# Causal attention on one Trainium2 core: query-side scores in two pairs of PSUM banks, six row maxima a head, the split of the maximum on GpSimd

## The chip, the core and the metric

The kernel runs on one core of a Trainium2 chip. The metric is device time in microseconds (us); three runs of the kernel before gave 2903.61, 2900.68 and 2903.25, so the median is 2903.25. Engines are named as in the profile: PE is TensorE's matrix multiplication, PEld its weight load, DVE VectorE, ACT ScalarE, POOL GpSimd, SP SyncE.

## The reference, cut to what matters

The model is a convolution-style block (linear attention and an MLP), a causal softmax attention, and a feed-forward block with grouped quantization. The change touches the attention alone. Its arithmetic is this:

```python
k = (x @ Wk).reshape(B, H, T, hs)     # B = 32, H = 6, T = 1024, hs = 16
q = (x @ Wq).reshape(B, H, T, hs)
v = (x @ Wv).reshape(B, H, T, hs)
wei = jnp.einsum('bhtd,bhsd->bhts', q, k) * scale
wei = jnp.where(mask, wei, -jnp.inf)
wei = jax.nn.softmax(wei, axis=-1)
out = jnp.einsum('bhts,bhsd->bhtd', wei, v).reshape(B, T, C)
```

That is 192 heads of 1024 rows and 16 columns. A head is cut into 8 blocks of 128 rows; below and on the diagonal there are 36 blocks of 128 x 128 scores.

## The kernel before, in words

The program has a preparation, `conv_block`, `causal_attention` and `project_and_ffn`, one after the other. In `causal_attention` each head's scores are computed twice. First **on the query side**: rows are queries, and DVE takes the maximum of each row straight from PSUM. The negated maximum is split into two bf16 parts (high part and rest), turned by PE, copied by ACT and sent by a DMA into two spare rows of the queries' stack. Then **on the key side**: rows are keys, the two spare rows subtract the maximum inside the matmul, ACT takes the exponential from PSUM into SBUF, and PE multiplies with the values.

Every engine runs the same software pipeline, written out by hand: a `body(i)` for the iteration i, in which the stages of different heads stand together; heads are i for loading and spreading (POOL), i-2 for the query side (PE, DVE), i-3 for turning the maximum, i-4 and i-5 for the key side, i-5 for the output. The loop body is six iterations long (`SLOTS`). 190 iterations hold both a head's query side and a head's key side. Inside a `body`, PE goes through nine steps u = 0 to 8:

- Query units (`QUNITS`, line 853 in the profile): twelve a head. A unit is one PSUM bank of `at_ps_queries`: a strip of up to 512 keys for one query block, or four diagonal blocks followed by one matmul of 512 columns that adds the mask (line 857). `QSTEP` gives the step of each: 1, 2, 2, 3, 4, 4, 5, 6, 6, 7, 7, 8. The text calls the units Q0 to Q11. There are four banks (`QBANKS`); a unit waits until DVE has reduced the unit four before it (`unit_max`).
- Key units (line 868): nine a head, K0 to K8, one a step, in two banks (`KBANKS`). The key unit of a step is the last thing in it. K0 and K1 are the diagonal, K2 to K5 are one matmul of 512 columns each, K6 to K8 two matmuls with 512 together. In iteration i, steps 2 to 8 do K0 to K6 of head i-4, and steps 0 and 1 of the next iteration K7 and K8 of it. A key unit waits until ACT has done the exponential (`probs`, line 928) of the unit two before it. 
- Values (line 888): a batch of five units at step 0 and one of four at step 4.
- The turning of the maxima (line 834) at step 2 and of the output (line 843) at step 8, ahead of K6. The second waits for ACT's copy of the output (line 937), which ACT does after the exponential of K3.

DVE goes through the twelve units in order (one `tensor_reduce` each, line 982); before the last one it divides the output of head i-5 (lines 969 and 972); after it come the maximum over the parts (line 986) and the split (lines 990 and 992). POOL waits for the head's rows (`at_stacks`), spreads them (lines 803 to 816) and masks the diagonal probabilities of head i-4 (lines 820 and 822). SP issues the DMAs in order: rows of head i once head i-1 is spread, the transposing DMA of head i-1, the maximum's rows, the output's two.

Of the kernel before, what the change touches and what calls it, by code (L numbers as in the profile page):

```python
# [8 lines left out]
ALU = mybir.AluOpType  # L9
# [674 lines left out]
def causal_attention(nc, w, rows, rows_stored, att):  # L684
# [11 lines left out]
    WIDE = NU - DIAG  # L696
    SLOTS = 6
    BATCHES = {4: (0, 1, 2, 3, 4), 8: (5, 6, 7, 8)}
    QBANKS, KBANKS = 4, 2
    QDIAG = [[(qb, qb * P, P) for qb in range(g, g + HALF)] for g in (0, HALF)]  # L700
    QUNITS = [[(1, 0, P)], [(2, 0, 2 * P)], QDIAG[0], [(4, 0, BANK)], [(5, 0, BANK)], [(3, 0, 3 * P)], [(6, 0, BANK)],
              [(5, BANK, P)], QDIAG[1], [(7, BANK, 3 * P)], [(6, BANK, 2 * P)], [(7, 0, BANK)]]
    NQ = len(QUNITS)
    QSTEP = [1, 2, 2, 3, 4, 4, 5, 6, 6, 7, 7, 8]
    LAG = 11
    VALUES_LAG = 14
    MAX_TURN, MAX_COPY, OUT_COPY, OUT_TURN = 2, 3, 5, 8
    OUT_QUNIT = 11
    VW = 32
    with ExitStack() as ctx:  # L710
        def sb(name, shape, dt=FP32):
# [2 lines left out]
        def pb(name, shape, dt=FP32):  # L714
            return ctx.enter_context(nc.psum_tensor("at_ps_" + name, shape, dt))
# [21 lines left out]
        ONE = sb("one", [P, 1, 1])  # L737
        OT = sb("out_t", [P, 2 * P])
        AT = sb("att", [P, SLOTS, TILES, HD])
        pq = pb("queries", [P, QBANKS, BANK])  # L740
        pk = pb("keys", [P, KBANKS, BANK])
        pv = pb("values", [P, 2 * P])
        bank = pb("turn", [P, BANK])
# [12 lines left out]
        with nc.Block() as block:  # L756
# [30 lines left out]
            def _(pool):  # L787
# [7 lines left out]
                pool.wait_ge(S["one_set"], 1)  # L795

                def body(i, r, lap, on):
                    if on(0):
                        pool.wait_ge(loaded[r], _dmas(lap, r, 0, SLOTS))
                        _above(pool.wait_ge, S["values"], NU * (i - SLOTS + 1))  # L800
                        _above(pool.wait_ge, turned_in[r], _dmas(lap, r, SLOTS, SLOTS))
                        v = ST[:, r, :, PW:PW + HD].bitcast(FP32)
                        pool.tensor_tensor(V[:, r, :, 0:HD], v, ONE[:, :, :].broadcast_to([P, TILES, HD]), ALU.mult)  # L803
                        k, q = ST[:, r, :, 0:PW], ST[:, r, :, PW + HD:PACK]
                        ks, qs = (SPREAD[:, r, m, :, 0:STACK].bitcast(U32) for m in range(2))
                        h = HD // 2
                        pool.tensor_copy(ks[:, :, 0:3 * h], k)
                        pool.tensor_copy(ks[:, :, 3 * h:5 * h], k[:, :, 0:2 * h])
                        pool.tensor_copy(ks[:, :, 5 * h:6 * h], k[:, :, 0:h])
                        pool.tensor_copy(qs[:, :, 0:3 * h].rearrange("p t (m d) -> p t m d", m=3),  # L810
                                         q[:, :, 0:h].rearrange("p t (m d) -> p t m d", m=1)
                                         .broadcast_to([P, TILES, 3, h]))
                        pool.tensor_copy(qs[:, :, 3 * h:5 * h].rearrange("p t (m d) -> p t m d", m=2),
                                         q[:, :, h:2 * h].rearrange("p t (m d) -> p t m d", m=1)
                                         .broadcast_to([P, TILES, 2, h]))
                        pool.tensor_copy(qs[:, :, 5 * h:6 * h], q[:, :, 2 * h:3 * h]).then_inc(S["spread"], 1)
# [11 lines left out]
            def _(pe):  # L828
# [17 lines left out]
                def query_scores(h, r, lap, u):  # L846
                    slot = (r - 2) % SLOTS
                    if u == 0:
                        pe.wait_ge(turned_in[slot], _dmas(lap, r, 2, SLOTS))
                    _above(pe.wait_ge, S["unit_max"], NQ * h + u - QBANKS + 1)  # L850
                    c0 = 0
                    for qb, k0, n in QUNITS[u]:
                        mm = pe.matmul(pq[:, u % QBANKS, c0:c0 + n], QT[0:STACK, slot, qb * P:(qb + 1) * P],  # L853
                                       KT[0:STACK, slot, k0:k0 + n], start=(c0 == 0), stop=True, skip_group_check=True)
                        c0 += n
                    if len(QUNITS[u]) > 1:
                        mm = pe.matmul(pq[:, u % QBANKS, :], w["ident_bf"][:, :], w["mask_queries"][:, :],
                                       start=False, stop=True, skip_group_check=True)
                    mm.then_inc(S["q_scores"], 1)

                def key_scores(h, slot, lands, u):
# [79 lines left out]
            def _(dve):  # L941
# [20 lines left out]
                dve.tensor_tensor(w["w2"][:, :, 0:GROUPS * gs2], A2[:, :, :], B2[:, :, :], ALU.subtract)  # L962

                def body(i, r, lap, on):
                    for u, blocks in enumerate(QUNITS):
                        if u == OUT_QUNIT and on(5):
                            q = (r - 5) % SLOTS
                            dve.wait_ge(S["out_turned"], i - 4)
                            dve.reciprocal(RC[:, :], out_ps[:, :, HD]).then_inc(S["recip"], 1)
                            dve.wait_ge(S["recip"], i - 4)  # L970
                            _above(dve.wait_ge, stored[q], 2 * _dmas(lap, r, 5 + SLOTS, SLOTS))
                            dve.tensor_tensor(AT[:, q, :, :], out_ps[:, :, 0:HD], _bcast(RC[:, :], 2, HD),
                                              ALU.mult).then_inc(S["out_ready"], 1)
                        if on(2):
                            dve.wait_ge(S["q_scores"], NQ * (i - 2) + u + 1)
                            qb, k0, n = blocks[0]
                            if len(blocks) > 1:
                                peaks, scores = MX[:, r % 2, qb:qb + len(blocks), 2], pq[:, u % QBANKS, :].rearrange(
                                    "p (t n) -> p t n", n=P)
                            else:  # L980
                                peaks, scores = MX[:, r % 2, qb, k0 // BANK:k0 // BANK + 1], pq[:, u % QBANKS, 0:n]
                            dve.tensor_reduce(peaks, scores, AX.X, ALU.max).then_inc(S["unit_max"], 1)  # L982
                    if on(2):
                        dve.wait_ge(S["unit_max"], NQ * (i - 1))
                        _above(dve.wait_ge, S["max_parts"], i - 2)
                        dve.tensor_reduce(NM[:, :], MX[:, r % 2, :, :], AX.X, ALU.max,
                                          negate=True).then_inc(S["head_max"], 1)
                        dve.wait_ge(S["head_max"], i - 1)
                        _above(dve.wait_ge, S["max_turned"], i - 3)
                        dve.tensor_copy(MP[:, r % 2, 0:TILES], NM[:, :]).then_inc(S["max_high"], 1)  # L990
                        dve.wait_ge(S["max_high"], i - 1)
                        dve.tensor_tensor(MP[:, r % 2, TILES:2 * TILES], NM[:, :], MP[:, r % 2, 0:TILES],
                                          ALU.subtract).then_inc(S["max_parts"], 1)
                _pipeline(dve, body, NHEADS, 7, SLOTS)


# [426 lines left out]
```

## Time and profile before

| | |
|---|---|
| median of three runs | 2903.25 us |
| span of the profiled execution | 2901.5 us |
| attention (query side of the first head to the values of the last) | about 1009 to 2424 us of the span |
| PE busy / PEld / DVE / ACT / POOL, whole span | 94% / 58% / 79% / 70% / 40% |
| one head in the middle of the attention | 7.285 us (1100 us hold 151 heads) |

The profile is of one execution. Busy shares are those of instruction records. The records of PE overlap: matmuls are pipelined, so the distance between the starts of two matmuls tells how long one holds the array, and its duration in the record (0.38 us for 512 columns) is longer than that (0.22 us). Idle time in front of an instruction is shown with the instruction that ended it. A few per cent of the matmul records are missing, among them nearly all of the mask matmul, line 857.

### The profile page before, as it was taken

To read this page: it belongs to the slowest core of one execution; us is meant where nothing else is said; L and a number is where in the kernel's file an instruction comes from. 1 tells how busy PE (TensorE), PEld (TensorE's weight loads), DVE (VectorE), ACT (ScalarE), POOL (GpSimd) and SP (SyncE) were. 2 spreads that over 40 slices of the span, in tenths; PEclk is the share of its full clock that TensorE was granted. 3 is DMA by queue.
4 is the path that set the end of the run, shared out by engine and by line. 5 is a ranking of instruction groups with operands and counts; after the bars stand their busy time and mean duration, and the time that the engine had idled before them with its cause. 6 is when DMAs were issued, how large, how long until landed. Compare 5 with 4: busy or idle time off the path is not lost. (4 is left out here: it accounts for less than half of the span.)

```text
span 2901.5 us, 86028 instructions
## 1 busy us (share of the span) xinstructions
PE 2730.6 (94%) x28924; PEld 1685.7 (58%) x29306; DVE 2300.3 (79%) x4585; ACT 2020.8 (70%) x3943; POOL 1153.0 (40%) x1999
## 2 busy tenths in 40 slices
PE   4999999999999499999999999999999997899996
PEld 2555555555554266666666666666666664455553
DVE  3577676676765499999999999999999994678997
ACT  2677777777776267777777777777777774577775
POOL 1144443444434434444444444444444441224445
PEclk9999999999999699999999999999999998999998
DMA  1113223232332466666666666666666663334555
GB/s 34 44 55 115 90 100 114 76 114 85 105 114 85 128 118 119 116 118 118 118 118 118 118 118 118 118 117 117 117 117 117 118 117 86 99 105 132 147 142 154
DMA packets 923408, 316.04 MB, mean 109 GB/s; under 512 B 848785, under 2 KB 906418, under 8 KB 923314
## 3 DMA queue, kind: packets, MB, share of 16 engines
q1 hardware_dynamic: 921970, 313.59, 47.8%
q8 instruction: 60, 0.98, 0.1%
q10 hardware_dynamic: 1344, 1.18, 0.1%
q14 instruction: 34, 0.28, 0.0%
HBM read 113.35 MB, written 99.88 MB: 73 GB/s over the span
## 5 line engine op out<-in xcount | busy, mean ns | idle before, releaser
L982 DVE TENSOR_REDUCE at_unit_max<-at_ps_queries 128x1 f32<-128x512 f32 (+4 forms) x2304 | 1135.9, 550 | 86.0 <-PE at_ps_queries L853 83.5
L928 ACT ACTIVATE at_probs<-at_ps_keys 128x512 f32<-128x512 f32 x1344 | 743.3, 603 | 388.9 <-PE at_ps_keys L868 384.5
L853 PE MATMUL at_ps_queries<-at_turned 96*128 96x128 bf16 (+3 forms) x3456 | 635.1, 275 | 30.6 <-DMA at_turned<-at_spread 29.4
L868 PE MATMUL at_ps_keys<-at_turned 128*128 128x128 bf16 x3453 | 648.4, 275 | 13.3 <-ACT at_probs L928 1.7
L803 POOL TENSOR_TENSOR at_v<-at_stacks,at_one 128x128 f32<-128x128 f32 x192 | 76.7, 399 | 818.5 <-DMA at_stacks<-qkv_rows 818.5
L888 PE MATMUL at_ps_values<-at_probs,at_v 128*32 128x128 f32 x10752 | 373.4, 276 | 6.5 <-ACT at_probs L928 6.5
L868 PEld LDWEIGHTS at_ps_keys<-at_turned 128*128 128x128 bf16 x3456 | 238.0, 97 | 239.5 <-ACT at_probs L928 88.3
L853 PEld LDWEIGHTS at_ps_queries<-at_turned 96*128 96x128 bf16 x3456 | 289.7, 98 | 122.0 <-DMA at_turned<-at_spread 31.3
L888 PEld LDWEIGHTS at_ps_values<-at_probs,at_v 128*32 128x32 f32 x10752 | 269.5, 109 | 120.6 <-ACT at_diag_probs L928 70.2
L928 ACT ACTIVATE at_diag_probs<-at_ps_keys 128x512 f32<-128x512 f32 x384 | 208.7, 595 | 8.5 <-PE at_ps_keys L868 5.6
L822 POOL TENSOR_SCALAR_AFFINE_SELECT at_diag_probs<-at_diag_probs 128x1024 f32<-128x1024 f32 x192 | 210.3, 1095 | 0.0
L576 PE MATMUL cb_ps_hidden<-cb_xn_t,fc 96*128 96x512 f32 x384 | 186.2, 615 | 8.4 <-ACT cb_hidden_t L557 8.4
L487 POOL TENSOR_TENSOR cb_o_hat<-cb_o,cb_o_scale 128x768 f32<-128x768 f32 x32 | 48.1, 1502 | 357.0 <-DVE cb_o_scale L403 357.0
L637 PE MATMUL cb_ps_out<-cb_hidden_t,fc 128*96 128x512 f32 x384 | 176.2, 594 | 0.0
L1121 PE MATMUL ff_ps_hidden<-ff_xn_t,w 97*128 97x512 f32 x360 | 171.0, 609 | 1.8 <-ACT ff_xn_t L1236 1.8
L557 ACT ACTIVATE cb_hidden_t<-cb_ps_hidden,fc_bias 128x512 f32<-128x512 f32 x192 | 128.5, 686 | 59.3 <-PE cb_ps_hidden L576 58.9
L1210 ACT ACTIVATE ff_hidden<-ff_ps_hidden 128x512 f32<-128x512 f32 x180 | 104.6, 597 | 93.2 <-PE ff_ps_hidden L1121 93.2
L467 DVE SCALAR_TENSOR_TENSOR cb_o<-cb_q_norm_v,cb_ps_hidden 128x768 f32<-128x768 f32 x32 | 30.6, 955 | 165.8 <-PE cb_ps_hidden L663 165.8
L1273 POOL TENSOR_TENSOR ff_scale<-ff_var_sums,ff_minus_half 128x8 f32<-128x8 f32 x30 | 49.5, 1650 | 247.0 <-DVE ff_var_sums L1359 247.0
L1313 DVE TENSOR_REDUCE ff_max<-ff_hidden 128x1 f32<-128x1024 f32 x90 | 109.5, 1217 | 36.3 <-ACT ff_hidden L1210 36.3
L576 PEld LDWEIGHTS cb_ps_hidden<-cb_xn_t,fc 96*128 96x128 f32 x384 | 66.1, 193 | 101.2 <-ACT cb_hidden_t L557 71.4
L637 PEld LDWEIGHTS cb_ps_out<-cb_hidden_t,fc 128*96 128x96 f32 x384 | 62.9, 164 | 102.0 <-issue 102.0
(214 smaller groups left out, 4967.4 us busy)
## 6 DMA issues: line engine op xcount, KB each, us to landing
qkv_rows<-cb_packed SPq DMA_DIRECT2D x32, 1536.0 KB, 8.3
at_stacks<-qkv_rows SPq DMA_DIRECT2D x192, 256.0 KB, 3.3
cb_x<-in_x_dram SPq DMA_DIRECT2D x32, 384.0 KB, 3.7
cb_x_again<-in_x_dram SPq DMA_DIRECT2D x32, 384.0 KB, 4.5
x_after_conv<-cb_x SPq DMA_DIRECT2D x32, 384.0 KB, 5.0
attention_rows<-at_att SPq DMA_DIRECT2D x384, 32.0 KB, 2.2
ff_att_rows<-attention_rows SPq DMA_DIRECT2D x32, 384.0 KB, 4.5
ff_x<-x_after_conv SPq DMA_DIRECT2D x128, 96.0 KB, 2.4
```

The lines of the kernel that those rows point to most:

```text
L557: act.activation(HT[:, r, k, a * BANK:(a + 1) * BANK], pf[:, a * BANK:(a + 1) * BANK], ACT.Silu, bias=w["fc1_bias"][:, k:k + 1]).then_inc( ...
L576: pe.matmul(pf[:, a * BANK:(a + 1) * BANK], w["fc1"][:, k * P:(k + 1) * P], XNT[:, a * BANK:(a + 1) * BANK], start=True, stop=True).then_i ...
L637: pe.matmul(po[0:C, half], w["fc2"][:, k, :], HT[:, q, k, half], start=(k == 0), stop=False)
L822: pool.affine_select(out=blocks, in_=blocks, compare_op=ALU.is_ge, fill=0.0, base=0, pattern=[[0, TILES], [1, P]], channel_multiplier=-1). ...
L853: mm = pe.matmul(pq[:, u % QBANKS, c0:c0 + n], QT[0:STACK, slot, qb * P:(qb + 1) * P], KT[0:STACK, slot, k0:k0 + n], start=(c0 == 0), stop ...
L868: mm = pe.matmul(pk[:, bank_k, c0:c0 + n * P], KT[:, slot, kb * P:(kb + 1) * P], QT[:, slot, q0 * P:(q0 + n) * P], start=(c0 == 0), stop=True,
L888: mm = pe.matmul(pv[row:row + VW, col:col + P], V[:, slot, kb, :], probs[:, c0:c0 + P], start=(v == 0), stop=True, skip_group_check=True)
L928: act.activation(probs, pk[:, (slot * NU + k) % KBANKS, :], ACT.Exp, scale=scale).then_inc(S["probs"], 1)
L982: dve.tensor_reduce(peaks, scores, AX.X, ALU.max).then_inc(S["unit_max"], 1)
L1121: pe.matmul(pf[:, a * BANK:(a + 1) * BANK], w["w1"][:, k * P:(k + 1) * P], XNT[:, a * BANK:(a + 1) * BANK], start=True, stop=True).then_in ...
L1210: act.activation(Y1[:, n % SLOTS1, k, a * BANK:(a + 1) * BANK], pf[:, a * BANK:(a + 1) * BANK], ACT.Copy).then_inc(S["y1_copied"], 1)
L1313: dve.tensor_reduce(G1[:, n // GB % 2, c:c + 1], Y1[:, n % SLOTS1, k, :], AX.X, ALU.max, apply_absolute_value=True).then_inc(S["y1_max"], 1)
```

## The change

The query units become five, Q0 to Q4, each in a pair of neighbouring banks (1024 columns), and there are two pairs. Q0 holds all eight diagonal blocks with both masks, Q1 the first 512 keys of query blocks 4 and 5, Q2 those of 6 and 7, Q3 the mixed strips (384 + 128 in each bank), Q4 256 and 256. Their steps are 0, 0, 1, 3, 5. A unit waits until the unit two before it is reduced. DVE reduces four units with one instruction each and Q3 with two. DVE's split moves to POOL, as the first thing of the next iteration (for head i-3), and the division of the output moves behind the maximum over the parts.

```diff
-    QBANKS, KBANKS = 4, 2
+    QPAIRS, KBANKS = 2, 2
-    QUNITS = [[(1, 0, P)], [(2, 0, 2 * P)], QDIAG[0], [(4, 0, BANK)], [(5, 0, BANK)], [(3, 0, 3 * P)], [(6, 0, BANK)],
-              [(5, BANK, P)], QDIAG[1], [(7, BANK, 3 * P)], [(6, BANK, 2 * P)], [(7, 0, BANK)]]
+    QUNITS = [QDIAG, [[(4, 0, BANK)], [(5, 0, BANK)]], [[(6, 0, BANK)], [(7, 0, BANK)]],
+              [[(3, 0, 3 * P), (1, 0, P)], [(7, BANK, 3 * P), (5, BANK, P)]], [[(2, 0, 2 * P), (6, BANK, 2 * P)]]]
+    QMAXIMA = [[(0, 8, 1, 2, P, 0, P)], [(4, 6, 1, 0, BANK, 0, BANK)], [(6, 8, 1, 0, BANK, 0, BANK)],
+               [(3, 8, 4, 1, BANK, 0, 3 * P), (1, 6, 4, 1, BANK, 3 * P, P)], [(2, 7, 4, 1, 2 * P, 0, 2 * P)]]
-    QSTEP = [1, 2, 2, 3, 4, 4, 5, 6, 6, 7, 7, 8]
+    QSTEP = [0, 0, 1, 3, 5]
...
@@ pool body @@
+                    if on(3):
+                        q = (r - 3) % SLOTS % 2
+                        pool.wait_ge(S["head_max"], i - 2)
+                        _above(pool.wait_ge, S["max_turned"], i - 4)
+                        pool.tensor_tensor(MP[:, q, 0:TILES], NM[:, :], ONE[:, :, 0].broadcast_to([P, TILES]), ALU.mult
+                                           ).then_inc(S["max_high"], 1)
+                        pool.wait_ge(S["max_high"], i - 2)
+                        pool.tensor_tensor(MP[:, q, TILES:2 * TILES], NM[:, :], MP[:, q, 0:TILES],
+                                           ALU.subtract).then_inc(S["max_parts"], 1)
...
@@ query_scores on PE @@
-                    _above(pe.wait_ge, S["unit_max"], NQ * h + u - QBANKS + 1)
+                    before = MAXDONE[u - QPAIRS] if u >= QPAIRS else MAXDONE[u - QPAIRS + NQ] - NMAX
+                    _above(pe.wait_ge, S["unit_max"], NMAX * h + before)
+                    pair = pq[:, (NQ * r + u) % QPAIRS, :]
...
@@ dve body @@
-                        dve.wait_ge(S["head_max"], i - 1)
-                        _above(dve.wait_ge, S["max_turned"], i - 3)
-                        dve.tensor_copy(MP[:, r % 2, 0:TILES], NM[:, :]).then_inc(S["max_high"], 1)
-                        dve.wait_ge(S["max_high"], i - 1)
-                        dve.tensor_tensor(MP[:, r % 2, TILES:2 * TILES], NM[:, :], MP[:, r % 2, 0:TILES],
-                                          ALU.subtract).then_inc(S["max_parts"], 1)
+                    if on(5):
+                        q = (r - 5) % SLOTS
+                        dve.wait_ge(S["out_turned"], i - 4)
+                        dve.reciprocal(RC[:, :], out_ps[:, :, HD]).then_inc(S["recip"], 1)
...
```

**PE, steps 5 to 8 of an iteration.** In the kernel before, from K3 to the first matmul of K6 (`at_ps_keys` at line 868 is a key unit, `at_ps_queries` at line 853 a query unit, `at_ps_turn` the turned output):

```order
L868 MATMUL at_ps_keys<-at_turned 128x512 [waits at_probs]
L853 MATMUL at_ps_queries<-at_turned 128x128 [waits at_unit_max] x2
L853 MATMUL at_ps_queries<-at_turned 128x128 x3
L857 MATMUL at_ps_queries<-mask_queries,ident_bf 128x512
L868 MATMUL at_ps_keys<-at_turned 128x512 [waits at_probs]
L853 MATMUL at_ps_queries<-at_turned 128x384 [waits at_unit_max]
L853 MATMUL at_ps_queries<-at_turned 128x256 [waits at_unit_max]
L868 MATMUL at_ps_keys<-at_turned 128x512 [waits at_probs]
L853 MATMUL at_ps_queries<-at_turned 128x512 [waits at_unit_max]
L843 MATMUL at_ps_turn<-ident,at_out_t 128x128 [waits at_max_copied,at_out_ready,at_out_copied]
L843 MATMUL at_ps_turn<-ident,at_out_t 128x128
L868 MATMUL at_ps_keys<-at_turned 128x384 [waits at_probs]
```

The same place now, from K2 on (line 884 is a key unit, 868 a query unit, 855 the turned output):

```order
L884 MATMUL at_ps_keys<-at_turned 128x512 [waits at_probs]
L868 MATMUL at_ps_queries<-at_turned 128x256 [waits at_unit_max]
L868 MATMUL at_ps_queries<-at_turned 128x256
L884 MATMUL at_ps_keys<-at_turned 128x512 [waits at_probs] x3
L855 MATMUL at_ps_turn<-ident,at_out_t 128x128 [waits at_max_copied,at_out_ready,at_out_copied]
L855 MATMUL at_ps_turn<-ident,at_out_t 128x128
L884 MATMUL at_ps_keys<-at_turned 128x384 [waits at_probs]
L884 MATMUL at_ps_keys<-at_turned 128x128
```

The query matmuls that stood between K3, K4, K5 and K6 are gone from there, and K3, K4 and K5 follow each other; the query matmuls stand at steps 0, 1 and 3 now.

**DVE, one head.** Before, the row maxima (line 982), the output (969, 972), the maximum over the parts (986) and the split (990, 992):

```order
L982 TENSOR_REDUCE at_unit_max<-at_ps_queries 128x1 [waits at_q_scores] x2
L982 TENSOR_REDUCE at_unit_max<-at_ps_queries 128x4 [waits at_q_scores]
L982 TENSOR_REDUCE at_unit_max<-at_ps_queries 128x1 [waits at_q_scores] x5
L982 TENSOR_REDUCE at_unit_max<-at_ps_queries 128x4 [waits at_q_scores]
L982 TENSOR_REDUCE at_unit_max<-at_ps_queries 128x1 [waits at_q_scores] x2
L969 RECIPROCAL at_recip<-at_ps_turn 128x8 [waits at_out_turned]
L972 TENSOR_TENSOR at_att<-at_ps_turn,at_recip 128x128 [waits at_recip]
L982 TENSOR_REDUCE at_unit_max<-at_ps_queries 128x1 [waits at_q_scores]
L986 TENSOR_REDUCE at_neg_max<-at_unit_max 128x8 [waits at_max_parts,at_unit_max]
L990 CAST at_max_parts<-at_neg_max 128x8 [waits at_max_turned,at_head_max]
L992 TENSOR_TENSOR at_max_parts<-at_neg_max,at_max_parts 128x8 [waits at_max_high]
```

Now, one head on DVE:

```order
L989 TENSOR_REDUCE at_unit_max<-at_ps_queries 128x8 [waits at_q_scores]
L989 TENSOR_REDUCE at_unit_max<-at_ps_queries 128x2 [waits at_q_scores] x3
L989 TENSOR_REDUCE at_unit_max<-at_ps_queries 128x2
L989 TENSOR_REDUCE at_unit_max<-at_ps_queries 128x2 [waits at_q_scores]
L993 TENSOR_REDUCE at_neg_max<-at_unit_max 128x8 [waits at_max_parts,at_unit_max]
L998 RECIPROCAL at_recip<-at_ps_turn 128x8 [waits at_out_turned]
L1001 TENSOR_TENSOR at_att<-at_ps_turn,at_recip 128x128 [waits at_stored1,at_recip]
```

Twelve reductions became six, the two instructions of the split left the engine, and the output's two stand behind the maximum over the parts.

## Rows read from the trace of the kernel before

**Rows 1.** Busy time by engine, 1200 to 2300 us: the middle of the attention.

```profile
core 0: us, PE busy (x) PEld busy (x) DVE busy (x) ACT busy (x) POOL busy (x), PEclk, DMA share, GB/s
1200.00:2300.00 1100.00, 1077.53 (x16740) 725.62 (x17033) 1009.65 (x2566) 791.32 (x1659) 451.35 (x1355) 1.00 0.64 117
```

**Rows 2.** Who waited for whom, 1200 to 2300 us: total, times, longest.

```profile
POOL at_v L803 <- DMA at_stacks<-qkv_rows: 648.6, 151, 5.0
...
PEld at_ps_keys L868 <- ACT at_probs L928: 70.5, 376, 0.2
DVE at_unit_max L982 <- PE at_ps_queries L853: 60.3, 176, 0.4
```

**Rows 3.** Timeline of PE over one head: start, length, line, tile, form, count.

```profile
1623.61 0.39 PE L868 MATMUL at_ps_keys<-at_turned 128*128 128x512 bf16 x1
1623.84 0.38 PE L853 MATMUL at_ps_queries<-at_turned 96*128 96x512 bf16 x1
1624.06 0.38 PE L868 MATMUL at_ps_keys<-at_turned 128*128 128x512 bf16 x1
1624.28 0.44 PE L853 MATMUL at_ps_queries<-at_turned 96*128 96x128 bf16 x5
1624.78 0.38 PE L868 MATMUL at_ps_keys<-at_turned 128*128 128x512 bf16 x1
1624.99 0.43 PE L853 MATMUL at_ps_queries<-at_turned 96*128 96x384 bf16 x2
1625.26 0.38 PE L868 MATMUL at_ps_keys<-at_turned 128*128 128x512 bf16 x1
1625.48 0.38 PE L853 MATMUL at_ps_queries<-at_turned 96*128 96x512 bf16 x1
1625.70 0.38 PE L843 MATMUL at_ps_turn<-ident,at_out_t 128*128 128x128 f32 x2
1625.94 0.39 PE L868 MATMUL at_ps_keys<-at_turned 128*128 128x384 bf16 x2
1626.27 1.30 PE L888 MATMUL at_ps_values<-at_probs,at_v 128*32 128x128 f32 x40
1627.50 0.39 PE L868 MATMUL at_ps_keys<-at_turned 128*128 128x256 bf16 x2
...
1628.56 0.22 PE L834 MATMUL at_ps_turn<-ident_bf,at_max_parts 128*128 128x128 bf16 x1
1628.61 0.39 PE L868 MATMUL at_ps_keys<-at_turned 128*128 128x128 bf16 x4
...
1630.79 0.39 PE L868 MATMUL at_ps_keys<-at_turned 128*128 128x512 bf16 x1
```

**Rows 4.** Timeline of ACT over the same head.

```profile
1624.04 1.09 ACT L928 ACTIVATE at_probs<-at_ps_keys 128x512 f32<-128x512 f32 x2 [0.97 <-PE at_ps_keys L868]
1625.01 0.39 ACT L937 ACTIVATE at_out_t<-at_ps_values 128x256 f32<-128x256 f32 x1
1625.27 1.70 ACT L928 ACTIVATE at_probs<-at_ps_keys 128x512 f32<-128x512 f32 x3
1627.92 1.09 ACT L928 ACTIVATE at_probs<-at_ps_keys 128x512 f32<-128x512 f32 x2 [0.96 <-PE at_ps_keys L868]
```

**Rows 5.** Two heads earlier, timelines of ACT and PEld: the exponential of K2, the load for K4.

```profile
1609.45 1.09 ACT L928 ACTIVATE at_probs<-at_ps_keys 128x512 f32<-128x512 f32 x2 [1.06 <-PE at_ps_keys L868]
...
1610.10 0.10 PEld L868 LDWEIGHTS at_ps_keys<-at_turned 128*128 128x128 bf16 x1 [0.18 <-ACT at_probs L928]
```

**Rows 6.** DVE by form, 1200 to 2300 us: busy us, mean ns, idle before.

```profile
L982 DVE TENSOR_REDUCE at_unit_max<-at_ps_queries 128x1 f32<-128x512 f32 x603 | 399.4, 683 | 51.2 <-PE at_ps_queries L853 51.2
...
L982 DVE TENSOR_REDUCE at_unit_max<-at_ps_queries 128x1 f32<-128x128 f32 x302 | 86.3, 286 | 9.1 <-PE at_ps_queries L853 9.1
```

**Rows 7.** Timeline of DVE: five reductions of 1792 columns together, then the reciprocal.

```profile
1624.26 2.28 DVE L982 TENSOR_REDUCE at_unit_max<-at_ps_queries 128x1 f32<-128x512 f32 x5 [0.40 <-PE at_ps_queries L853]
1626.45 0.20 DVE L969 RECIPROCAL at_recip<-at_ps_turn 128x8 f32<-128x8 f32 x1
```

**Rows 8.** Timeline of POOL over the same head: two of its small operations.

```profile
1621.87 0.40 POOL L803 TENSOR_TENSOR at_v<-at_stacks,at_one 128x128 f32<-128x128 f32 x1 [4.30 <-DMA at_stacks<-qkv_rows]
...
1623.63 0.20 POOL L820 TENSOR_TENSOR at_tick<-at_one 128x1 f32<-128x1 f32 x1
```

**Rows 9.** Busy time and granted clock, 985 to 1015 us: the start of the attention.

```profile
985.00:1015.00 30.00, 5.78 (x25) 2.63 (x27) 14.15 (x42) 0.00 (x0) 13.11 (x28) 0.50 0.62 168
```

## What I predicted before the run

> **What bounds the kernel now.** I first read the busy times over the middle of the attention [rows 1]. The reader is to see two engines near their limit: PE at 1077.5 of 1100 us and DVE at 1009.7. ACT has 791 and POOL 451. POOL waits for the rows of a head 151 times in that stretch, once a head [rows 2], so a head takes 1100 / 151 = 7.285 us. All of this change that can matter is what it does to that number, 190 times (the iterations that have both a query side and a key side).
>
> Which of the two engines sets it? The list of waits says so [rows 2]: DVE stood waiting for PE's query scores for 60.3 us, while no row has PE waiting for DVE; PE's weight loads waited for ACT's exponentials for 70.5 us, at most 0.2 at a time, much of it hidden under the matmul that was still running. So PE leads, DVE follows with 0.4 us of air a head, and the only engine that ever holds PE is ACT.
>
> Then I read PE by its starts [rows 3]. A matmul of 512 columns holds the array for 0.22 us (1623.84 to 1624.06). From K2 (1623.61) to the next head's K2 (1630.79) are 7.18 us, and in them the starts follow each other without a hole: such a head is pure PE work. The mean is 0.1 above it. So **PE can gain about 0.1 us a head at most, whatever DVE is spared**, and it can lose as much as its waits grow.
>
> Where is PE nearly waiting? Between K2 and K6 [rows 3, 4]. ACT begins the exponential of K2 at 1624.04, that of K3 0.49 later (two take 1.09, so one is 0.60 long), then copies the output (1625.01 to 1625.40), then that of K4 at 1625.27, which ends 0.60 later at 1625.87. K6 needs that last one, because there are two key banks, and K6 starts at 1625.94. How fast PE goes on after an exponential is seen two heads earlier [rows 5]: exponential of K2 from 1609.45 to 1610.05, load for K4 at 1610.10, so 0.05 us. **ACT needs 2.31 us from the start of K2 to that of K6** (0.43 + 0.49 + 0.49 + 0.25 + 0.60 + 0.05), and PE's own work between them takes 2.33 (1625.94 - 1623.61). The two are even: PE's query matmuls just fill the time that ACT needs for its exponentials.
>
> **The change part by part.**
>
> *The same matmuls, in another order.* The query side has 36 blocks and two masks before and after, so PE's work stays at 7.18 us a head. What moves is where it stands. Between K2 and K6 the kernel before had Q6, then Q7 and Q8 with its mask (1624.28 to 1624.78, 0.50), Q9 and Q10 (1624.99 to 1625.26, 0.27), Q11 (1625.48 to 1625.70, 0.22) [rows 3]. Now only Q4 stands there, with the 512 columns that Q6 had. So 0.50 + 0.27 + 0.22 = **0.99 us of PE's work leaves this stretch**. What is left in it is 2.33 - 0.99 = 1.34 us, but ACT still needs 2.31. Counted from K2's start, PE is at K4 at 0.67 and may start at 1.08 (exponential of K2: 0.43 + 0.60 + 0.05); K5 may start at 1.57, the turned output at 1.84 (copy ends at 1.79), K6 at 2.31. Four holes, of 0.41, 0.27, 0.05 and 0.23 us, together 0.97 but for rounding (2.31 - 1.34). The stretch stays at 2.3 us with a hole of 0.97, and the 0.99 are added to the rest of the head, which was solid PE work before (4.85 us from K6 to the next K2). Nothing there has air to take them: **+0.99 us a head**.
>
> *K0 after the second query pair.* ACT starts on K7 0.42 after K7's start (1627.50, 1627.92) [rows 3, 4], ends 0.60 later, and K0 may go 0.05 after that: 1.07. PE now gets there after K7 (0.22), Q2 (0.44), K8 (0.22) and the turned maximum (0.05 to 0.10) [rows 3]: 0.93 to 0.98. That is a new hole of about 0.09 us; before, the way from K7 to K0 took 1.11. Where ACT begins 0.09 later, as it did at 1609.45 [rows 5], it is 0.18. Lower end 0. I take **+0.09**.
>
> *Six reductions fewer, the split gone from DVE.* A reduction of 512 columns lasts 683 ns and one of 128 lasts 286 [rows 6], so a column costs 1.03 ns. Five with 1792 columns took 1626.45 - 1624.26 = 2.19 us from start to start [rows 7]; less 1792 x 1.03 = 1.85 leaves 0.34, so what each instruction adds is 0.07 us, not the 0.15 that its record seems to say, since the records overlap. Six fewer free 0.4 us of DVE, and the two small ones of the split some tenths more. All of it lies on an engine that was waiting already. Worth: 0.
>
> *Two pairs in the place of four banks.* This adds waits of PE for DVE, so I follow one. Q0 holds PE for 2048 columns, 0.88 us; its scores are seen 0.16 later (0.38 - 0.22) and DVE starts 0.04 after that (Q6: 1623.84 + 0.38, DVE at 1624.26) [rows 3, 7]. A reduction of 1024 columns isn't in this stage; from 683 ns and 1.03 a column it is 1.21 us. So Q0 is reduced at 0.88 + 0.16 + 0.04 + 1.21 = 2.29. Q2, which needs that pair, comes after Q1 (0.44), the batch of five values (1626.27 to 1627.50, 1.23) and K7 (0.22): at 2.77. It has 0.48 us of air. Q1 is reduced 1.14 later, at 3.43, and Q3 comes at 2.77 + 0.44 + 0.22 + 0.1 + 0.3 = 3.8. Q4 and the next Q0 have over a microsecond. Worth: 0; from below it can't be a gain, since no PE wait for DVE was there; from above, see the rivals.
>
> *The split on POOL.* Two operations on 128x8; the nearest rows are 0.20 us for 128x1 and 0.40 for 128x128 [rows 8], so 0.4 to 0.8 with the wait between them. They stand at the head of POOL's iteration, before the spreading of the next head, where POOL has waited 4.3 us for the rows from memory [rows 2, 8]. Queued behind the new wait are the spreading, SP's transposing DMA after it, and the diagonal mask that the values wait for. DVE's maximum over the parts is ready about a step after Q4, well before the rows land. PE turns the maximum at step 2 of the next iteration, over 3 us later. Worth: 0, with that wait of 4.3 us as cover.
>
> *The division behind the maximum.* On DVE, which has air: 0.
>
> **Sum.** 0.99 + 0.09 = 1.08 us a head; 190 heads give +205 us. Against the profiled execution, 2901.5 + 205 = 3106.5, and the median stands 1.75 above its span: 3108. The fill of the pipeline, where DVE alone is slow, gives back a microsecond or two: **3106 us**. Bounds of this case: if the holes between K2 and K6 are a tenth smaller and K0 has none, 0.90 a head, 3074; if ACT is late at each place (0.18 at K0, and a few hundredths at each of the hand-overs), 1.25, 3141.
>
> **The rivals.**
>
> *DVE was the bound, and the kernel gets faster.* For it: DVE is busy 92% of the time and its chain gets shorter by well over half a microsecond. The Trainium skill ("Perfetto Trace Analysis", "Identifying the Most-Contended Engine") says that matmul busy time isn't a fair measure of TensorE and the share of weight loads is, while a busy share is fair for VectorE; by that rule DVE with 92% would stand ahead of PE with 66% of weight loads [rows 1], and the change would pay. Against it: DVE waits for PE and never PE for DVE. Its price: PE's own 7.18 us stays, so at most 0.1 a head is gained, 190 x 0.1 = 20 us, 2883. It also needs the holes at K4 to K6 not to come. Chance 0.06.
>
> *The change does nothing to the time.* If ACT got to its exponentials sooner than I read, or if what I call solid work between K6 and K2 had a microsecond of air in it, the two would cancel: 2898 to 2909. The starts in rows 3 speak against the air. Chance 0.04.
>
> *Half of it.* ACT is busy 72% of the time only, so some of the holes may close by a shift that I don't see: +0.5 us a head, 2998. Chance 0.04.
>
> *The pairs bind as well.* If a reduction over two banks takes longer than 1.21 us by more than the 0.48 of air (eight groups of 128, or strips with a step of 512, might go slower than a single bank), PE waits at Q2 and Q3 too: half a microsecond a head on top, 3106 + 95 = 3200. Chance 0.04.
>
> *The clock falls.* At the start of the attention, where PE was busy 5.8 of 30 us, the granted clock is 0.50, so 1.2 GHz; in the middle it is 1.00, 2.4 GHz [rows 1, 9]. Now PE would have holes of half a microsecond again and again. One head in eight at half the clock would cost 7 / 8 of a microsecond a head, +165, 3270. The Trainium skill ("TensorE: Matmul & The Clock Gate", "A second HAM failure mode: psum-queue depth-cycling") tells of a kernel whose small pauses between groups of matmuls in cycling PSUM banks made the clock go back and forth; by that rule this case would be likelier than I make it. The holes are short beside 24 us of idleness in rows 9. Chance 0.02.
>
> **How the numbers follow.** Forecast 0.80, DVE bound 0.06, no change 0.04, half 0.04, pairs 0.04, clock 0.02. The range holds the forecast's bounds, 3074 to 3141, with some more below for holes that partly close, down to 3060, and 3145 above; the rivals, 0.20 in all, are outside. Faster by over 0.2%: 0.06; within 0.2%, about what a measurement can tell from no change: 0.04; slower: 0.90.
>
> **What would show it.** In the new profile a head in the middle of the attention should last about 8.36 us; PE should have holes ahead of K4, K5 and K6 ended by ACT's exponentials, together near a microsecond; DVE's waits for PE should grow from 0.4 us to nearly 2 a head, its busy share fall to about 70%; a reduction of 1024 columns should last 1.21 us; ACT's stretch from the exponential of K2 to that of K4 should keep its 1.23 us; POOL's two new operations should have no one waiting for them; the granted clock should stay at 1.00. I am wrong if PE waits for `at_unit_max`, if K4 comes without a hole, or if the time from K6 to the next K2 stays near 4.9 us and doesn't grow to 5.9.

## The result, and the profile after

The changed kernel takes 3120.59 us (median of four runs, 3119.75 to 3121.93); the kernel before, run beside it, 2901.97. The ratio is 1.0753, with a 95% interval of 1.0738 to 1.0768: slower by 7.5%. The forecast was 3106 us, with a range of 3060 to 3145. The span of the profiled execution is 3118.9 us, 217.4 more than before.

The first two views are of the changed kernel, 1200 to 2300 us, and answer to [rows 1, 2]: busy time by engine, and who waited for whom (total us, times, longest).

```profile
1200.00:2300.00 1100.00, 1014.96 (x14654) 619.07 (x14785) 806.52 (x1175) 699.58 (x1436) 448.49 (x1437) 1.00 0.56 102
```

```profile
POOL at_v L815 <- DMA at_stacks<-qkv_rows: 492.5, 131, 4.4
...
PEld at_ps_keys L884 <- ACT at_probs L944: 214.3, 521, 0.7
DVE at_unit_max L989 <- PE at_ps_queries L873: 107.3, 131, 1.1
DVE at_recip L998 <- PE at_ps_turn L855: 103.0, 130, 0.9
POOL at_max_parts L805 <- DVE at_neg_max L993: 86.1, 130, 0.7
...
DVE at_unit_max L989 <- PE at_ps_queries L868: 60.9, 130, 0.5
...
PE at_ps_queries L868 <- DVE at_unit_max L989: 20.6, 130, 0.2
```

POOL's wait comes 131 times where it came 151 times, so a head takes 1100 / 131 = 8.4 us in place of 7.285. DVE fell from 92% to 73% busy and waits three times a head (107.3 + 103.0 + 60.9 = 271 us, 2.1 a head, where it was 0.4). The weight loads of the key units wait three times as long for ACT (214.3 us against 70.5). The clock is 1.00 as before.

A finer measure, which the experiments below use too: the view of one tile gives the first and the last turned maximum, 191 heads apart. Before they are at 1015.9 and 2408.3, so a head is 7.29 us; now at 1019.7 and 2624.9, **8.40 us**, 1.11 more. 191 x 1.114 = 213 of the 217 us lie there. The lengths of single heads repeat every six heads: most often 7.18 us before (up to 7.50), most often 8.29 now (up to 8.68). The timelines show one head of the shortest kind in each kernel.

Where in the head? Timeline of PE over one head, against [rows 3] (start, length, line, tile, form, count; line 884 is a key unit, 868 a query unit, 873 the mask, 904 values, 855 the turned output, 846 the turned maximum):

```profile
1626.91 0.38 PE L868 MATMUL at_ps_queries<-at_turned 96*128 96x256 bf16 x2 [0.16 <-DVE at_unit_max L989]
1627.13 0.38 PE L884 MATMUL at_ps_keys<-at_turned 128*128 128x512 bf16 x1
1627.76 0.88 PE L884 MATMUL at_ps_keys<-at_turned 128*128 128x512 bf16 x2 [0.25 <-ACT at_probs L944]
1628.53 0.44 PE L855 MATMUL at_ps_turn<-ident,at_out_t 128*128 128x128 f32 x2
1629.02 0.39 PE L884 MATMUL at_ps_keys<-at_turned 128*128 128x384 bf16 x2
...
1631.89 0.39 PE L884 MATMUL at_ps_keys<-at_turned 128*128 128x256 bf16 x2
1632.12 0.60 PE L868 MATMUL at_ps_queries<-at_turned 96*128 96x512 bf16 x2
1632.56 0.38 PE L884 MATMUL at_ps_keys<-at_turned 128*128 128x128 bf16 x2
1632.78 0.22 PE L846 MATMUL at_ps_turn<-ident_bf,at_max_parts 128*128 128x128 bf16 x1
1632.97 0.40 PE L884 MATMUL at_ps_keys<-at_turned 128*128 128x128 bf16 x4
...
1635.20 0.39 PE L868 MATMUL at_ps_queries<-at_turned 96*128 96x256 bf16 x2 [0.16 <-DVE at_unit_max L989]
```

The weight loads of the same stretch, with the idle time before each; the first is K2's:

```profile
1626.68 0.10 PEld L884 LDWEIGHTS at_ps_keys<-at_turned 128*128 128x128 bf16 x1 [0.20 <-issue]
...
1627.76 0.10 PEld L884 LDWEIGHTS at_ps_keys<-at_turned 128*128 128x128 bf16 x1 [0.64 <-ACT at_probs L944]
1628.25 0.10 PEld L884 LDWEIGHTS at_ps_keys<-at_turned 128*128 128x128 bf16 x1 [0.39 <-ACT at_probs L944]
1628.53 0.20 PEld L855 LDWEIGHTS at_ps_turn<-ident,at_out_t 128*128 128x128 f32 x2 [0.18 <-ACT at_out_t L953]
1629.02 0.11 PEld L884 LDWEIGHTS at_ps_keys<-at_turned 128*128 128x128 bf16 x2 [0.29 <-ACT at_probs L944]
```

And ACT, against [rows 4]:

```profile
1627.11 1.08 ACT L944 ACTIVATE at_probs<-at_ps_keys 128x512 f32<-128x512 f32 x2 [0.59 <-PE at_ps_keys L884]
1628.08 0.39 ACT L953 ACTIVATE at_out_t<-at_ps_values 128x256 f32<-128x256 f32 x1
1628.35 1.70 ACT L944 ACTIVATE at_probs<-at_ps_keys 128x512 f32<-128x512 f32 x3
```

K2's matmul has no record here, but its weight load stands at 1626.68, 0.23 ahead of Q4 as in [rows 3]; ACT begins on it 0.43 later, as before. That also explains the "0.16 <-DVE" at Q4, and with it the one row of the list in which PE seems to wait for DVE (20.6 us): the gap is the missing matmul, not a wait. From the starts: PE is done with K3 at 1627.35 and starts K4 at 1627.76, a hole of 0.41; K5 follows at 1628.25, a hole of 0.27; the turned output at 1628.53, 0.06; K6 at 1629.02, 0.25. **Together 0.99 us of holes, each ended by ACT.** K2 to K6 takes 2.34 us, as before (2.33). From K6 to the next K2 (its load is at 1634.97) it is 5.95, where it was 4.85.

### The profile page after: what moved, and what is told of

It reads as the page before. It is cut to its first block and busy times, and to the rows that moved or that the text cites. A ratio compares the mean times of both kernels' runs of the same rounds, so it can differ in the third digit from the quotient of the medians.

```text
span 3118.9 us, 82755 instructions
## 1 busy us (share of the span) xinstructions
PE 2849.3 (91%) x29113; PEld 1670.1 (54%) x29306; DVE 2196.9 (70%) x3049; ACT 2042.0 (65%) x3943; POOL 1236.3 (40%) x2383
## 5 line engine op out<-in xcount | busy, mean ns | idle before, releaser
L989 DVE TENSOR_REDUCE at_unit_max<-at_ps_queries 128x2 f32<-128x1024 f32 (+4 forms) x1152 | 1054.8, 955 | 269.4 <-PE at_ps_queries L873 168.4
L944 ACT ACTIVATE at_probs<-at_ps_keys 128x512 f32<-128x512 f32 x1344 | 764.1, 604 | 579.4 <-PE at_ps_keys L884 564.7
L884 PE MATMUL at_ps_keys<-at_turned 128*128 128x128 bf16 (+3 forms) x3264 | 597.5, 269 | 90.6 <-ACT at_probs L944 54.5
L868 PE MATMUL at_ps_queries<-at_turned 96*128 96x128 bf16 (+3 forms) x3456 | 573.2, 274 | 69.2 <-DVE at_unit_max L989 33.1
L868 PEld LDWEIGHTS at_ps_queries<-at_turned 96*128 96x128 bf16 x3456 | 282.1, 98 | 153.3 <-DMA at_turned<-at_spread 31.0
L944 ACT ACTIVATE at_diag_probs<-at_ps_keys 128x512 f32<-128x512 f32 x384 | 228.2, 595 | 9.8 <-PE at_ps_keys L884 6.4
L998 DVE RECIPROCAL at_recip<-at_ps_turn 128x8 f32<-128x8 f32 x192 | 39.9, 208 | 166.5 <-PE at_ps_turn L855 166.5
L873 PE MATMUL at_ps_queries<-mask_queries,ident_bf 128*128 128x512 bf16 x383 | 147.2, 384 | 0.0
```

Of the source, the lines that this page charges most:

```text
L868: mm = pe.matmul(pair[:, c0:c0 + n], QT[0:STACK, slot, qb * P:(qb + 1) * P], KT[0:STACK, slot, k0:k0 + n], start=(c0 == b * BANK), stop=Tr ...
L873: mm = pe.matmul(pair[:, b * BANK:(b + 1) * BANK], w["ident_bf"][:, :], w["mask_queries"][:, :], start=False, stop=True, skip_group_check= ...
L884: mm = pe.matmul(pk[:, bank_k, c0:c0 + n * P], KT[:, slot, kb * P:(kb + 1) * P], QT[:, slot, q0 * P:(q0 + n) * P], start=(c0 == 0), stop=True,
L944: act.activation(probs, pk[:, (slot * NU + k) % KBANKS, :], ACT.Exp, scale=scale).then_inc(S["probs"], 1)
L989: dve.tensor_reduce(MX[:, r % 2, first:last:every, part], scores, AX.X, ALU.max).then_inc(S["unit_max"], 1)
```

## The experiments

For each, "a head" is the distance between the first and the last turned maximum over 191; the kernel before has 7.29, the changed one 8.40. Ratios are to the kernel before, on the same chip.

### The changed kernel's order in the kernel before (e2)

```diff
-    QSTEP = [1, 2, 2, 3, 4, 4, 5, 6, 6, 7, 7, 8]
+    QSTEP = [0, 0, 0, 0, 1, 1, 2, 3, 3, 4, 4, 5]
```

> The kernel before (four banks, twelve reductions, split on DVE) with one table altered: the steps of the twelve query units become 0, 0, 0, 0, 1, 1, 2, 3, 3, 4, 4, 5, so that only one unit of 512 columns stands between K2 and K6, as in the changed kernel. Theory: the same holes come at K4, K5, K6, a head lasts about 8.3 to 8.4 us, the kernel 3090 to 3125. Rival (pairs, fewer instructions or POOL's split are what costs): it stays near 2902, at most 1% above.

Measured: 3207.88 us, ratio 1.1054 (1.1036 to 1.1072), a head 8.88. With four banks, twelve reductions and the split on DVE the loss is there, and larger. Timeline of PE (line 868 is now the key unit, 853 the query unit, 888 values):

```profile
1701.78 0.39 PE L868 MATMUL at_ps_keys<-at_turned 128*128 128x512 bf16 x1
1702.01 0.38 PE L853 MATMUL at_ps_queries<-at_turned 96*128 96x512 bf16 x1
1702.23 0.38 PE L868 MATMUL at_ps_keys<-at_turned 128*128 128x512 bf16 x1
1702.86 0.88 PE L868 MATMUL at_ps_keys<-at_turned 128*128 128x512 bf16 x2 [0.25 <-ACT at_probs L928]
1703.62 0.44 PE L843 MATMUL at_ps_turn<-ident,at_out_t 128*128 128x128 f32 x2
1704.12 0.39 PE L868 MATMUL at_ps_keys<-at_turned 128*128 128x384 bf16 x2
1704.34 0.55 PE L853 MATMUL at_ps_queries<-at_turned 96*128 96x128 bf16 x6
1705.29 0.39 PE L853 MATMUL at_ps_queries<-at_turned 96*128 96x512 bf16 x1 [0.39 <-DVE at_unit_max L982]
```

K2 to K6 is the same picture: 2.34 us (1701.78 to 1704.12), K4 0.41 late. The last row is what the expectation missed: PE waits for DVE. Counted by columns (Q0 to Q2 and the mask, whose matmul has no record, are 0.61 us) PE is ready for Q3 at 1704.95 and starts it at 1705.29, a hole of 0.34. The bank of Q3 is the one that Q11 of the head before had. The timeline of DVE shows why it isn't free:

```profile
1704.10 0.21 DVE L969 RECIPROCAL at_recip<-at_ps_turn 128x8 f32<-128x8 f32 x1 [2.01 <-PE at_ps_turn L843]
...
1704.55 0.68 DVE L982 TENSOR_REDUCE at_unit_max<-at_ps_queries 128x1 f32<-128x512 f32 x1
```

DVE was not short of time: it stood idle for 2.01 us. In the kernel before, the division of the output stands ahead of the last unit's reduction, and it waits for the turned output at step 8. Q11 was finished at step 5, but DVE reduces it only behind the division, until 1705.23, and Q3 goes on 0.05 later. Eleven reductions then stand in a row on DVE, and a second wait of PE for it comes at step 4 (the load at 1700.55 waited 0.32). The changed kernel has the division behind the maximum and shows no such wait; the division's place was not tested alone. The theory's size was 0.5 us a head too small, its sign and place were right.

### The pairs, with the steps spread (e1)

```diff
-    QSTEP = [0, 0, 1, 3, 5]
+    QSTEP = [1, 3, 5, 7, 8]
```

> The changed kernel with one table altered: the query units go to steps 1, 3, 5, 7, 8 in place of 0, 0, 1, 3, 5. Theory (ACT paces K2 to K6 and the query work that filled this stretch is gone): the stretch gets 1.10 us of query work back in place of 0.22, K4's hole shrinks from 0.4 to about 0.2, and about 0.2 us of a new wait for DVE comes at Q4; a head should last about 7.55 us in place of 8.43, the kernel about 2950 to 2980. Rival (two pairs in place of four banks, or the split on POOL, make the loss): the order does not matter much and the time stays within 1% of 3120.

Measured: 2986.84 us, ratio 1.0290 (1.0272 to 1.0308), a head 7.72. One table gives back 134 of the 219 us. It is 7 us above the upper end that was expected. The two holes that were expected are there, about 0.2 us at K4 (K3's 0.22 ends at 1705.81, K4's load is at 1706.00) and at Q4 0.18 for DVE (ready at 1706.89, started at 1707.07). The trace also shows a hole that was left out, at K1. Timelines of PE and ACT:

```profile
1702.94 0.60 PE L868 MATMUL at_ps_queries<-at_turned 96*128 96x512 bf16 x2
1703.59 0.40 PE L884 MATMUL at_ps_keys<-at_turned 128*128 128x128 bf16 x4
```

```profile
1702.94 0.60 ACT L944 ACTIVATE at_probs<-at_ps_keys 128x512 f32<-128x512 f32 x1 [0.51 <-PE at_ps_keys L884]
```

Q1 is through at 1703.38, K1 starts at 1703.59, 0.05 after the exponential of K8 ends (1703.54). The whole diagonal, 0.88 us, stood between K7 and K8 and made that exponential late.

### Shorter exponentials (e4)

```diff
-                            act.activation(probs, pk[:, (slot * NU + k) % KBANKS, :], ACT.Exp,
+                            n = BANK if k < DIAG else BANK // 2
+                            act.activation(probs[:, 0:n], pk[:, (slot * NU + k) % KBANKS, 0:n], ACT.Exp,
```

> The changed kernel with ACT's exponentials of K2 to K8 over 256 of their 512 columns (the other half is left out and its place in SBUF holds a constant, so this part of the softmax is not computed). PE's work is unchanged. Theory (the holes are the chain of exponentials): an exponential of 256 columns should last 0.39 us in place of 0.60 and follow the one before after 0.26 in place of 0.49; K2 to K6 shrinks from 2.34 to about 1.85 us and K0's hole goes, so a head lasts 7.8 to 7.9 us and the kernel 3000 to 3025. Rival (PE's holes come from DVE, the banks or PE's own order): the time stays within 0.5% of 3120.

Measured: 2994.57 us, ratio 1.0317 (1.0300 to 1.0334), a head 7.74. But for one memset of DVE ahead of the loop, no PE or DVE instruction was altered, and 126 of the 219 us are gone. The time is 5 us below the range expected. Timeline of PE:

```profile
1703.88 0.39 PE L868 MATMUL at_ps_queries<-at_turned 96*128 96x256 bf16 x2 [0.16 <-DVE at_unit_max L992]
1704.11 1.32 PE L884 MATMUL at_ps_keys<-at_turned 128*128 128x512 bf16 x3
1705.32 0.44 PE L855 MATMUL at_ps_turn<-ident,at_out_t 128*128 128x128 f32 x2
1705.60 0.39 PE L884 MATMUL at_ps_keys<-at_turned 128*128 128x384 bf16 x2
```

K2 (0.23 ahead of the first row, 1703.65) to K6 is 1.95 us in this head. By the starts of the weight loads, as a mean over the heads of 1200 to 2300 us, K2 to K6 is 1.88 in place of 2.36, and from the turned maximum to K0 0.19 in place of 0.40; no other stretch of the head changed by more than 0.02. So the 0.66 us a head came back just where PE waited for exponentials, more of it at K0 than was expected.

### DVE's and POOL's parts, alone (e3, e6, e7)

e3 is the changed kernel with the split back on DVE; e7 is the changed kernel with the maxima of Q1 to Q4 taken bank by bank, eleven reductions a head; e6 is the kernel before with the split on POOL:

```diff
@@ e6: the kernel before @@
+                    if on(3):
+                        q = (r - 3) % SLOTS % 2
+                        pool.wait_ge(S["head_max"], i - 2)
...
-                        dve.tensor_copy(MP[:, r % 2, 0:TILES], NM[:, :]).then_inc(S["max_high"], 1)
```

```diff
@@ e7: the changed kernel @@
-    QMAXIMA = [[(0, 8, 1, 2, P, 0, P)], [(4, 6, 1, 0, BANK, 0, BANK)], [(6, 8, 1, 0, BANK, 0, BANK)],
+    QMAXIMA = [[(0, 8, 1, 2, P, 0, P)], [(4, 5, 1, 0, 2 * BANK, 0, BANK), (5, 6, 1, 0, 2 * BANK, BANK, BANK)],
...
```

> The changed kernel with the split of the maximum back on DVE, behind the maximum over the parts. Theory: the split is off the path in either place, so the time is that of the changed kernel, 3120, within 0.3%. Rival (POOL's wait for the maximum delays the spreading and by it the turned scores, or PE's turning of the maximum): the time falls by 1% or more, to 3090 or below.

> The kernel before with nothing but the split of the maximum moved to POOL, as in the change. Theory: DVE gets 0.3 to 0.5 us a head of air that nobody uses, 2890 to 2905, same within 0.3%. Rival 1 (DVE bounded the kernel before): faster by over 0.5%. Rival 2 (the split on POOL costs): slower by over 0.5%.

> The changed kernel with the row maxima of Q1 to Q4 taken bank by bank, so eleven reductions a head in place of six; pairs, waits and steps as they are. Theory: about 0.35 us more on DVE, which waits over 2 us a head, so no effect: 3120 within 0.3%. Rival (the number of reductions counts): slower by 0.35 us a head or more, 3185 or above.

Measured: e3 3118.30 us, ratio 1.0744 (1.0726 to 1.0762); e7 3119.55, 1.0749 (1.0733 to 1.0766); both are the changed kernel's 1.0753. e6 2902.14, 0.9998 (0.9989 to 1.0007), no change at all. So the place of the split moves the time in neither kernel, and the number of reductions doesn't move it in the changed one. (The division's new place on DVE was not tested alone.) What moves is the waits. In e7, the busy times of 1200 to 2300 us show that DVE took the five reductions more in its stride (845.57 us busy where it was 806.52, with PE as before):

```profile
1200.00:2300.00 1100.00, 1014.68 (x14654) 618.93 (x14777) 845.57 (x1830) 699.76 (x1437) 449.73 (x1439) 1.00 0.55 102
```

In e6, the waits of the same stretch show where the time went that DVE was spared, and what the cover of POOL's split is worth in the old order:

```profile
POOL at_max_parts L802 <- DVE at_neg_max L995: 462.2, 151, 3.4
...
POOL at_v L812 <- DMA at_stacks<-qkv_rows: 114.5, 151, 1.2
DVE at_unit_max L991 <- PE at_ps_queries L862: 90.4, 302, 0.4
```

DVE now waits 90.4 us for PE, where it was 60.3 [rows 2].

POOL now stands 3.1 us a head before the maximum, and of the 4.3 us that it waited for the rows 0.8 are left. The move costs nothing, but four fifths of the cover are used up.

### The pairs in an order that fits (e5, e8)

```diff
@@ e5: the changed kernel; the unit of 256 + 256 and that of query blocks 6 and 7 change places @@
-    QSTEP = [0, 0, 1, 3, 5]
+    QSTEP = [(1, 1), (3, 3), (5,), (6, 6), (7, 8)]
...
-                                if QSTEP[nq] == u:
-                                    query_scores(i - 2, r, lap, nq)
+                                for b, step in enumerate(QSTEP[nq]):
+                                    if step == u:
+                                        query_scores(i - 2, r, lap, nq, b)
@@ e8: e5, but @@
-    QSTEP = [(1, 1), (3, 3), (5,), (6, 6), (7, 8)]
+    QSTEP = [(1, 2), (3, 3), (5,), (6, 6), (7, 8)]
```

A pair's two banks may stand at different steps here; all else of the change is in place.

> The changed kernel with its pairs, its six reductions and POOL's split, but other steps: the order is diagonal (step 1), query blocks 4 and 5 (step 3), the unit of 256 + 256 (step 5), the mixed strips (step 6), query blocks 6 and 7 with one bank at step 7 and one at step 8. Theory: 1.10 us of query work stands between K2 and K6, in pieces of 0.22, 0.44, 0.22 and 0.22 that fit between ACT's exponentials, and no unit comes before DVE has freed its pair by more than 0.1 us; a head should last 7.2 to 7.4 us, the kernel 2885 to 2925, so the whole loss is gone with the pairs still in place. Rival (two pairs cost something of their own in any order): it stays above 2950.

> The reordered pairs (e5) with the diagonal's second bank moved from step 1 to step 2, behind K8. In e5 K1 had a hole of 0.14 us, because 0.88 us of diagonal ahead of K8 made the exponential of K8 late, on which K1 waits. Theory (what e5 still loses against the kernel before is order, not the pairs): that hole goes, 0.1 us a head, 2915 to 2930. Rival (the pairs' waits for DVE make the rest): DVE starts on the diagonal later, the waits at the pairs grow by as much, and the time stays at 2940 or above.

Measured: e5 2944.74 us, ratio 1.0146 (1.0130 to 1.0161), a head 7.51, above the expected range; e8 2913.16, ratio 1.0038 (1.0024 to 1.0051), a head 7.33, just below its range. In e5 the hole at K1 was there again, since the diagonal still stood ahead of K8. Timelines of PE and ACT in e5:

```profile
1701.85 0.60 PE L869 MATMUL at_ps_queries<-at_turned 96*128 96x512 bf16 x2
1702.43 0.40 PE L886 MATMUL at_ps_keys<-at_turned 128*128 128x128 bf16 x4
```

```profile
1701.78 0.60 ACT L947 ACTIVATE at_probs<-at_ps_keys 128x512 f32<-128x512 f32 x1 [0.51 <-PE at_ps_keys L886]
```

and the same two units of PE in e8, 0.43 apart, which is Q1's own 0.44:

```profile
1700.51 0.60 PE L869 MATMUL at_ps_queries<-at_turned 96*128 96x512 bf16 x2
1700.94 0.39 PE L886 MATMUL at_ps_keys<-at_turned 128*128 128x128 bf16 x4
```

So 208 of the 219 us came from the order. What is left of the whole change in e8, pairs, six reductions, split and division, is 0.4%, or 0.04 us a head. One small wait for DVE to free a pair can be seen in e5: from K4 (1704.87) to the next query bank are 0.30 us in place of 0.22, up to 1705.17. It costs nothing there: K2 to K6, in which it lies, takes 2.36 us as a mean (by the weight loads) in e5 and in e8, just as in the kernel before, since ACT's chain sets it. In e8 the 0.04 lie between K7 and the values of step 4, where 0.11 us more query work stands than before (1.10 us of it are between K2 and K6 in e8, 1.21 in the kernel before). So the rest, too, may be order; a cost of the pairs themselves isn't shown.

### Four banks, the smallest unit last (e9)

e9 is e6 with the unit of 128 columns moved from step 1 to step 8, behind the last unit.

```diff
-    QSTEP = [1, 2, 2, 3, 4, 4, 5, 6, 6, 7, 7, 8]
+    QSTEP = [2, 2, 3, 4, 4, 5, 6, 6, 7, 7, 8, 8]
```

> The kernel before with the split on POOL (e6) and its smallest query unit (query block 1, 128 columns) moved from step 1 to step 8, behind the last unit and ahead of K6. Theory (ACT's chain from K2 to K6 takes 2.31 or 2.40 us, PE's work 2.33 in between, so 0.05 us more work in the stretch fills the late heads' hole and takes as much from the rest): a gain of 0.03 us a head at most, less a new hole at K0 of up to 0.09: 2895 to 2915. Rival (the steps do not matter at this size): within 0.2% of 2902.

Measured: 2928.68 us, ratio 1.0094 (1.0078 to 1.0109), a head 7.43. It is worse than either expectation. By the weight loads (means over the heads of 1200 to 2300 us) all of the 0.14 us by which a head is longer than in e6 lies between K2 and the values of step 0: 2.87 us in place of 2.73. 0.055 of it is the work that came, the rest is waits, among them PE's loads for query units, which wait for DVE now, as in no row of the kernel before. And nothing came back where the work left: K7 to K0 takes 1.13 us, 1.12 in e6, since the exponential of K7 ends no sooner.

```profile
PEld at_ps_queries L862 <- DVE at_unit_max L991: 60.1, 147, 0.4
```

Moving 0.055 us of work from ahead of K8 to ahead of K6 costs almost three times as much. None of the kernels tried beats the kernel before.

## Why the prediction was right, point by point

**What bounds the kernel.** Right, and now shown for DVE: freeing it in the kernel before gives 0.9998 (e6), and loading it in the changed kernel costs nothing (e3, e7). That ACT holds PE is shown in the changed kernel (e4); for the kernel before it rests on the timelines and on the 2.36 us of the next paragraph. It is so in these orders: e1, e2 and e9 have PE waiting for DVE.

**K2 to K6 as the place.** Right in each number. The holes were forecast at 0.41, 0.27, 0.05 and 0.23 us and are 0.41, 0.27, 0.06 and 0.25; the stretch kept its 2.3 us. As a mean over the heads of 1200 to 2300 us, by the weight loads, K2 to K6 takes 2.36 us in the kernel before and in the changed one, and in e2, e3, e5, e6, e7 and e8 as well, with 0.22 us of query work in it or 1.21. It is longer where DVE holds PE inside it (e1 2.52, e9 2.43) and shorter only where the exponentials are (e4 1.88). e2 makes the loss with the order alone, and adds a wait for DVE to it; e1 and e8 undo most of it with the order alone; e4 undoes over half of it by making ACT faster.

**K0.** The hole was forecast at 0.09 us, with an upper end of 0.18. From K7 (1631.89) to the turned maximum (1632.78) PE works through, 0.89; with the turned maximum's 0.05 it would be at K0 at 0.94, and it starts at 1.08: 0.14. Three heads of every six have this, the other three 0.23, where ACT begins later; the mean is 0.18. So this term was half of what it measured, and its upper end was the mean.

**The sum.** Forecast 1.08 us a head on a mean of 7.285; measured 1.11. The head that was read in both traces went from 7.18 to 8.29. With K0's hole at 0.18 the terms would give 1.17; where the heads fall some 0.05 short of that wasn't followed, so a small part of the agreement is luck. Of the 14 us between 3106 and 3121, some 8 are the few hundredths a head, 4 lie outside the 191 heads, and 2 are those that the forecast took off for the fill of the pipeline. No run shows that gain: the first turned maximum comes at 1019.7 us of the span, where it was 1015.9.

**DVE's saving.** A reduction of 1024 columns lasts 1220 to 1225 ns, as the 1.21 us put together from [rows 6]. DVE's waits grew to 2.1 us a head ("nearly 2"), its busy share fell to 73% ("about 70%"). All of the saving went into waiting.

**Two pairs in the place of four banks.** Worth 0 in the order of the change: right. DVE starts on Q0 at 1630.33 and needs 1.22, so Q0 is reduced at 1631.55, and Q2 needs its pair at 1632.12: 0.57 us of air, forecast 0.48. In an order that fits ACT (e8) at most 0.4% is left of the whole change, and the trace doesn't put it on the hand-over to DVE.

**POOL.** POOL waited 0.66 us a head for DVE's maximum and 3.8 for the rows; nobody waited for its two operations, 0.20 us each. Right.

**The rivals.** DVE as the bound falls by e6. By the shares that the Trainium skill compares ("Perfetto Trace Analysis", "Identifying the Most-Contended Engine"), the busy share for VectorE and that of weight loads (one of its two measures) for TensorE, DVE would have come first; in this kernel the list of who waits for whom decided and the shares did not (e6). The falling clock didn't come: the granted clock stays at 1.00, so 2.4 GHz, with about a microsecond of holes in every head. "Half of it" falls too: ACT has air over the whole head but none between K2 and K6.

## What to carry to other kernels

Where one engine feeds another through two buffers in a fixed order, the feeder's other work is what fills the time that the consumer needs: before moving such work, measure the consumer's chain (here 0.49 us from one exponential to the next, 0.60 until its result counts) and check that each gap still has its piece. A consumer that is 72% busy can still set the pace in the third of the period in which all its work is asked for. And an engine at 92% was worth nothing to relieve here, since it was the one that waited (e6). Its own order counts all the same: in e2 a division that waited for PE stood ahead of a reduction that PE needed, and PE waited 0.34 us for a bank.

## What the runs showed of the hardware

Taking an fp32 reduction out of PSUM bank by bank or over two banks at once makes no difference but one instruction's start: 1220 ns for 1024 columns in one piece, 954 for 768 columns in strips of 384, and 1225 for 1024 in 8 x 128 form. The five reductions more of e7 cost DVE 845.57 - 806.52 = 39 us in 131 heads, 0.06 us each.

```profile
L989 DVE TENSOR_REDUCE at_unit_max<-at_ps_queries 128x2 f32<-128x1024 f32 x262 | 319.7, 1220 | 8.5
L989 DVE TENSOR_REDUCE at_unit_max<-at_ps_queries 128x8 f32<-128x1024 f32 x131 | 160.4, 1225 | 107.3 <-PE at_ps_queries L873 107.3
```

ACT does not start on a finished bank with one delay but with one of two, 0.43 us after the matmul's start (1627.11 here, 1624.04 in [rows 4]) or 0.52 (1609.45 in [rows 5], whose K2 started at 1608.93 in the trace); which heads get which repeats every six heads. Its cause wasn't looked for.
